# Expert stage: four expert outputs added onto x in one chain on VectorE instead of two accumulators and a join, with the routing set between the links

## What is computed

```python
def _L0_ffn_ref(x, router_w, router_b, expert_w, expert_b):
    router_probs = jax.nn.softmax(x @ router_w + router_b, axis=-1)
    top_p, top_i = jax.lax.top_k(router_probs, K)          # K = 2 of E = 8 experts
    top_p = top_p / jnp.sum(top_p, axis=-1, keepdims=True)
    expert_out = jnp.einsum('bnd,edc->bnec', x, expert_w) + expert_b
    gathered = jnp.take_along_axis(expert_out, top_i[..., None], axis=2)
    return jnp.einsum('bnk,bnkc->bnc', top_p, gathered)
...
t = t + _L0_ffn_ref(_ln_t(t), L0_ffn_router_w, L0_ffn_router_b, L0_ffn_expert_w, L0_ffn_expert_b)
```

## Time and profile before

| | before |
|---|---|
| median of 3 runs | 10527.13 us (10521.58 to 10538.14) |
| the profiled execution's own time | 10524.25 us |
| its span, first to last instruction | 10522.5 us |
| busy in the span: PE, DVE, ACT, POOL | 82%, 65%, 50%, 56% |
| the expert stage in it | about 2191 to 4327 us |
| busy in that stretch: PE, DVE, ACT, POOL | 1761, 1857, 1095, 1572 of 2136 us |

### The profile page before, as it was taken

The page is one execution under the profiler, slowest core; times in us unless marked ns, Lnnn a source line. Parts: engine busy times, 40 slices in busy tenths (PEclk is TensorE's granted clock), DMA queues, the critical chain, the costliest instruction groups (busy, mean ns, idle before and its releaser), DMA issues. The chain is left out here.

```text
span 10522.5 us, 333676 instructions
## 1 busy us (share of the span) xinstructions
PE 8609.7 (82%) x109757; PEld 5525.2 (53%) x109757; DVE 6874.4 (65%) x22569; ACT 5282.8 (50%) x14181; POOL 5917.0 (56%) x7369
## 2 busy tenths in 40 slices
PE   7888888878888888677759999995666668888888
PEld 5666666633333333355535555555666655555554
DVE  7888888878888888777725555556778772222222
ACT  4555555545555555566634444444666653333333
POOL 7777777767777777666612222224555554444444
PEclk9999999989999999888879999997888889999999
DMA  1111111111111111498943444437888862222222
GB/s 48 49 49 49 49 49 50 50 48 50 50 48 47 50 50 46 93 178 177 177 135 156 161 158 158 158 129 127 145 142 144 137 110 54 56 56 56 56 56 54
DMA packets 1199080, 961.46 MB, mean 91 GB/s; under 512 B 338169, under 2 KB 1078457, under 8 KB 1190202
## 3 DMA queue, kind: packets, MB, share of 16 engines
q1 hardware_dynamic: 1198522, 956.38, 36.8%
HBM read 576.97 MB, written 455.45 MB: 98 GB/s over the span
## 5 line engine op out<-in xcount | busy, mean ns | idle before, releaser
L943 PE MATMUL moe_pe_out<-moe_we,moe_xnT 128*128 128x512 f32 x3136 | 1531.6, 623 | 373.0 <-DVE moe_odd L836 197.2
L1533 PE MATMUL conv_pc<-conv_c,conv_toep 128*128 128x432 f32 (+1 forms) x3584 | 1370.5, 535 | 0.0
L740 ACT ACTIVATE moe_scaled<-moe_pe_out,moe_gate 128x128 f32<-128x128 f32 x3136 | 891.9, 367 | 867.6 <-PE moe_pe_out L943 865.8
L2092 ACT ACTIVATE rec_yT<-rec_ph 128x32 f32<-128x32 f32 x3136 | 618.5, 197 | 1241.7 <-PE rec_ph L2213 1241.7
L1384 POOL TENSOR_TENSOR conv_g<-conv_c,conv_gate 128x896 f32<-128x896 f32 x128 | 365.1, 2852 | 1462.9 <-DVE conv_out L1496 1362.8
L943 PEld LDWEIGHTS moe_pe_out<-moe_we,moe_xnT 128*128 128x128 f32 x3136 | 557.3, 195 | 1188.3 <-issue 1187.2
L2213 PE MATMUL rec_ph<-rec_yT,rec_vt 128*32 128x32 f32 x25080 | 843.1, 207 | 196.5 <-ACT rec_yT L2092 121.7
L1533 PEld LDWEIGHTS conv_pc<-conv_c,conv_toep 128*128 128x128 f32 x3584 | 672.1, 190 | 599.1 <-issue 599.1
L2139 DVE COPY rec_xT<-rec_pin 128x512 f32<-128x512 f32 x196 | 135.6, 692 | 1240.9 <-PE rec_pin L2185 1240.9
L281 POOL TENSOR_SCALAR att_xn<-att_xin,att_mv,att_rstd 128x128 f32<-128x128 f32 x1024 | 868.2, 857 | 54.1 <-POOL att_rstd L277 54.1
L678 POOL TENSOR_TENSOR moe_paired<-moe_scaled 128x256 f32<-128x256 f32 x784 | 569.3, 726 | 537.2 <-ACT moe_scaled L740 521.5
(11 more groups left out here) (194 smaller groups left out, 21904.3 us busy)
## 6 DMA issues: line engine op xcount, KB each, us to landing
conv_toep<-rows_dram SPq DMA_DIRECT2D x32, 2304.0 KB, 12.6
c<-foc_cs SPq DMA_DIRECT2D x32, 1856.0 KB, 12.0
conv_cin<-c SPq DMA_DIRECT2D x32, 1856.0 KB, 7.5
x<-att_x1s SPq DMA_DIRECT2D x3584, 14.0 KB
ctx_all<-conv_out SPq DMA_DIRECT2D x32, 1792.0 KB, 5.7
att_xin<-x_windows SPq DMA_DIRECT2D x512, 98.0 KB
moe_xin<-x SPq DMA_DIRECT2D x112, 448.0 KB, 3.5
x<-moe_acc SPq DMA_DIRECT2D x112, 448.0 KB, 2.7
```

What stands on the lines that cost most here:

```text
L740: ins = act.activation(scaled[:, b, e, :], pe_out[:, b, 1, e * C:(e + 1) * C], ACT.Identity, scale=g)
L943: ins = pe.matmul(pe_out[:, b, half, :], xnT[:, n.slot(2), t, :], we[:, half * 4:half * 4 + 4, :].rearrange("d e c -> d (e c)"), start=Tru ...
L1533: ins = pe.matmul(pc[k][:, half, 0:HALF * wide].rearrange("p (b i) -> p b i", i=wide)[:, :, i0:i1], w, tile[:, n.slot(slots), b, i0 + away ...
L2092: act.activation(yT[:, a, cs], ph[:, a, cs], ACT.Sigmoid).then_inc(moved, 1)
```

## The change

It takes away the accumulator `odd` and its join: experts 0, 1, 2, 3 are added onto x in `acc` one after another, each waiting for the one before with a `hold` on `mixing`. `add_others` of the tile before moves up, directly behind the first of the four. The 15 routing steps go one behind each of the four, from tile 2, place 0, on (k = 4(t-2)+place), and end in tile 5. ACT's `shares` moves from behind tile 2 to behind tile 3. The statistics of group n+3 are spread over the places of tile 6, and the rest of them follows it.

```diff
--- before.py
+++ after.py
@@ -588,7 +588,6 @@
         part = S.sb("part", [P, 2, T, E])
         gate = S.sb("gate", [P, 2, T, E])
         acc = S.sb("acc", [P, 4, T, C])
-        odd = S.sb("odd", [P, 2, C])
         scaled = S.sb("scaled", [P, 2, 4, C])
         paired = S.sb("paired", [P, 2, 2, C])
         others = S.sb("others", [P, 2, C])
@@ -610,7 +609,7 @@
         routing = S.sem("routing")
         shares_ready = S.sem("shares_ready")
         expert_done = S.sem("expert_done")
-        mixing, joined, mixed = S.sem("mixing"), S.sem("joined"), S.sem("mixed")
+        mixing, mixed = S.sem("mixing"), S.sem("mixed")
         scaled_ready, paired_ready, others_ready = S.sem("scaled_ready"), S.sem("paired_ready"), S.sem("others_ready")
         x2_out = S.sems("x2_out", 4)
         block = S.block()
@@ -752,7 +751,7 @@
                     if last < -1:
                         if t == 0:
                             front(n + 1, first)
-                        if t == 2:
+                        if t == 3:
                             shares(n + 1)
                     if t == 4 and last < -2:
                         norm(n + 2)
@@ -823,64 +822,45 @@
                     ins = dve.tensor_tensor(gate[:, n.slot(2), :, :], part[:, 0, :, :], part[:, 1, :, :], ALU.add)
                 ins.then_inc(routing, 1)
 
-            def route_between(n, t, place, more):
-
-                k = 6 * (t - 1) + place - 4
-                if more and 0 <= k < ROUTE_OPS:
+            def between(n, t, place, last):
+
+                k = 4 * (t - 2) + place
+                if last < -1 and 0 <= k < ROUTE_OPS:
                     route(n + 1, k)
-
-            def gated(n, t, e, into, start=False, onto=None):
-                g = gate[:, n.slot(2), t, e:e + 1]
-                src = pe_out[:, (n.off * T + t) % 2, 0, e * C:(e + 1) * C]
-                if start:
-                    dve.tensor_scalar(into, src, g, None, ALU.mult).then_inc(mixing, 1)
-                else:
-                    dve.scalar_tensor_tensor(out=into, in0=src, scalar=g, in1=into if onto is None else onto, op0=ALU.mult, op1=ALU.add)\
-                       .then_inc(mixing, 1)
-
-            def mix(n, t, first, more):
-
-
-                b = (n.off * T + t) % 2
-                if first >= 1 or t >= 2:
-                    hold(dve, joined, n.val(T, t - 1), ticks)
+                if last < -3 and t == T - 1:
+                    if place == 0:
+                        layer_stats(n + 3, 0, 1)
+                    layer_stats(n + 3, place + 1, place + 2)
+
+            def gated(n, t, e):
+                a = acc[:, n.slot(4), t, :]
+                dve.scalar_tensor_tensor(out=a, in0=pe_out[:, (n.off * T + t) % 2, 0, e * C:(e + 1) * C],
+                                         scalar=gate[:, n.slot(2), t, e:e + 1], in1=a if e else xin[:, n.slot(4), t, :],
+                                         op0=ALU.mult, op1=ALU.add).then_inc(mixing, 1)
+
+            def mix(n, t, first, last):
+
+
                 if t == 0:
                     hold(dve, routing, n.val(ROUTE_OPS, ROUTE_OPS), ticks)
+                    if first >= 4:
+                        hold(dve, x2_out[n.slot(4)], n.turn(4, 16), ticks)
                 dve.wait_ge(expert_done, n.val(T, t + 1))
-                gated(n, t, 1, odd[:, b, :], start=True)
-                route_between(n, t, 0, more)
-                if t == 0 and first >= 4:
-                    hold(dve, x2_out[n.slot(4)], n.turn(4, 16), ticks)
-                gated(n, t, 0, acc[:, n.slot(4), t, :], onto=xin[:, n.slot(4), t, :])
-                route_between(n, t, 1, more)
-                if first >= 1 or t >= 1:
-                    add_odd(n, t - 1)
-                route_between(n, t, 2, more)
-                hold(dve, mixing, n.val(T * MIX, MIX * t + 1), ticks)
-                gated(n, t, 3, odd[:, b, :])
-                route_between(n, t, 3, more)
-                if first >= 1 or t >= 1:
-                    add_others(n, t - 1)
-                route_between(n, t, 4, more)
-                hold(dve, mixing, n.val(T * MIX, MIX * t + 2), ticks)
-                gated(n, t, 2, acc[:, n.slot(4), t, :])
-                route_between(n, t, 5, more)
-
-            def tile_of(n, t):
+                for e in range(MIX):
+                    if e:
+                        hold(dve, mixing, n.val(T * MIX, MIX * t + e), ticks)
+                    gated(n, t, e)
+                    if e == 0 and (first >= 1 or t >= 1):
+                        add_others(n, t - 1)
+                    between(n, t, e, last)
+
+            def add_others(n, t):
 
                 m, u = (n, t) if t >= 0 else (n - 1, T - 1)
-                return acc[:, m.slot(4), u, :], (n.off * T + t) % 2
-
-            def add_odd(n, t):
-                a, b = tile_of(n, t)
+                a = acc[:, m.slot(4), u, :]
                 hold(dve, mixing, n.val(T * MIX, MIX * (t + 1)), ticks)
-                dve.tensor_tensor(a, a, odd[:, b, :], ALU.add).then_inc(joined, 1)
-
-            def add_others(n, t):
-                a, b = tile_of(n, t)
-                hold(dve, joined, n.val(T, t + 1), ticks)
                 dve.wait_ge(others_ready, n.val(T, t + 1))
-                dve.tensor_tensor(a, a, others[:, b, :], ALU.add).then_inc(mixed, 1)
+                dve.tensor_tensor(a, a, others[:, (n.off * T + t) % 2, :], ALU.add).then_inc(mixed, 1)
 
             def step(n, first, last):
                 if first == 0:
@@ -893,20 +873,15 @@
                         layer_stats_end(n + k)
                     for k in range(ROUTE_OPS):
                         route(n, k)
-                more = last < -1
                 for t in range(T):
-                    mix(n, t, first, more)
+                    mix(n, t, first, last)
                     if last < -2 and t == 2:
                         negate(n + 2)
-                    if last < -3 and t == 5:
-                        hold(dve, normed, n.val(TP, 2 * TP), ticks)
-                        layer_stats(n + 3, 0, 4)
-                    if last < -3 and t == 6:
-                        layer_stats(n + 3, 4, T)
-                if not more:
-                    add_odd(n, T - 1)
+                if last == -1:
                     add_others(n, T - 1)
                 if last < -3:
+                    layer_stats(n + 3, MIX + 1, T)
+                    hold(dve, normed, n.val(TP, 2 * TP), ticks)
                     layer_stats_end(n + 3)
 
             run_steps(dve, N, U, step, 4)
```

## The result

| | before | after |
|---|---|---|
| median | 10530.71 us (4 runs, 10521.58 to 10538.14) | 10756.29 us (4 runs, 10745.58 to 10759.79) |
| ratio, 95% interval | | 1.0213 [1.0195, 1.0231] |
| span of the profiled execution | 10522.5 us | 10752.9 us |
| expert stage, first expert matmul to last operation | 2137 us | 2360 us |
| the other five stages together, PE's first to last in each | 8123 us | 8134 us |

The kernel became 226 us slower, where 104 us were forecast. The sign and the first cause were right; the size was not, and 10756 us lies outside the range of 10504 to 10700. Nearly all of it is in the stage that was changed: of the 230 us between the two profiled executions 222 are there, and the other five stages grew by 11 together.

A forecast was written before the change was run, and what follows sets the result against it. A ring of PE, DVE's work and PE two tiles on bounds the expert stage. Groups of 19.05 against 18.18 us cost 97 us over 112, back edges 7; 104 on 10524 gives 10628 us, range 10504 to 10700.

The forecast's parts named there:

- the first cause: Expert stage, tiles 3 and 5: `add_others`, moved to second place, makes DVE wait for POOL's half, ready 3.30 us after ACT began.
- if L863 finds POOL's half ready in most tiles: Sign in the profile after that would prove the forecast wrong: `add_others` (L863) not waiting for POOL in most tiles.
- the pair that was named against rival B: Expert stage: DVE's busy time down by 220 us or more while the stage gets longer.
- rival B: DVE's load counts, so fewer operations make the kernel faster: group 16.25 us, 10308 us; chance 0.18 with partial forms.
- Links: DVE's chain of gated operations: each waits for the one before, 0.49 us start to start, bounds 0.37 and 0.49.
- rival A: Chained links cost only 0.26 us each, so the stage stays as long as now, 10518 to 10525 us; chance 0.12.
- The sum: One group from tile 2's matmuls: PE restarts at 13.52, plus 5.75 makes 19.27 us with both collisions; 19.05 taken against 18.18.
- I take the mean of the two ends of the second: Tile 5: step 12's collision with POOL's next addition, called close, counted at half, 19.27 less 0.22 us.
- The base: Group length before the change that the sum is compared with: 18.18 us, mean of three groups away from the back edge.
- At the 25 back edges DVE is late and its tile 0 is on the path: Loop's back edge: the chain needs 1.81 us where the alternation needed 1.52; 0.29 times 25, 7 us.
- Rival C: Worse than the sum: tile 6 holds PE up at the next group's tile 1, 10675 us and up; chance 0.12.
- The statistics and the moved sigmoids: Statistics only shift within and behind tile 6, thinly covered; sigmoids come one tile later, ACT's tile 4 0.22 us after they begin.

The follow-up runs named there:

- experiment 1: Kernel after with `add_others` moved from behind the first to behind the third of the four links: 10540.9 us, ratio 1.0017 to the kernel before.
- experiment 6: Kernel after with `add_others` behind the third link and the chain's waits bare instead of `hold`: 10439.4 us, ratio 0.9913 to the kernel before.
- experiment 7: Kernel after with four unused matmuls of 128 columns added on PE behind tiles 2 to 6: 10671.5 us, ratio 1.0135 to the kernel before.
- experiment 4: Kernel after with 40 increments of an unused counter ahead of DVE's loop, moving its code: 10724.9 us, ratio 1.0192 to the kernel before.
- experiment 2: Kernel after with the routing step put ahead of `add_others` instead of behind it: 10657.8 us, ratio 1.0128 to the kernel before.
- experiment 5: Kernel after with `add_others` behind the third link and 40 increments ahead of DVE's loop: 10632.0 us, ratio 1.0097 to the kernel before.

## Why the prediction was wrong in size

**The mechanism: right.** DVE waits for POOL's half in the tiles where that was forecast: 1.40 us a group, of which 0.85 in tile 5 and 0.35 in tile 3. It had not before, and moving `add_others` back takes nearly the whole loss away (experiment 1). One sign was badly put: "if L863 finds POOL's half ready in most tiles" would have made the forecast wrong, and it does find it ready in 503 of 784, but the forecast itself named two tiles of seven. DVE's busy time fell while the stage grew, the pair that was named against rival B; only the fall is 41 us and not 220, because an operation in a chain counts its whole length and because those that meet POOL's take up to 0.8 us. The forecast of that number had left both out. Experiments 1 and 6 show that rival B was no mere slip: with the late place the chain with fewer operations is indeed worth something, 38 us away from the edge and 91 in all with bare waits on top, but not 216, and not in the order that this change has.

**Links.** Taken at 0.49, measured at 0.50 with `hold` and 0.38 with the bare wait, which was the bound taken from below (0.37). So rival A, with links of 0.26, fell. The Trainium skill, VectorE: DVE Perf Modes, section on the drain that can't be avoided, has it that a semaphore after each operation costs nothing extra. The trace agrees for raising one: every gated operation here raises `mixing`, and an independent one still follows after 0.27 us (3014.92 to 3015.19 in the kernel after). The prediction took it for waits as well, and there the trace does not agree: even the bare wait for the operation before costs 0.12 us more than 0.26.

**The group: right in kind, too small.** The sum had 13.52 + 5.75, less 0.22 for half a collision, 19.05. The rows gave 13.69 + 5.87, so 19.56, and the collision of step 12 is there in full. The most frequent length over the stage is 19.53. That is 1.22 us above the 18.31 of before, times 87, 106 us, where the forecast had 0.87 x 87 = 76. Of the 0.51 us between 19.05 and 19.56 the step "I take the mean of the two ends of the second" is 0.22: in the rows above the end of POOL's half starts both engines' next additions within 0.1 us of each other, so that they meet is the rule here (107 of 112). The other 0.29 are 0.17 from tile 2 to PE's restart and 0.12 in tiles 0 and 1, which no step of the sum explains. The base was off too: the three groups of the earlier trace rows gave 18.18, the stage 18.31, which takes 0.13 back.

**The clock: not in the sum.** The mean of the 87 groups is not 19.53 but 19.97, since about a quarter of them last 21.13 like the one above. 0.44 x 87 is 38 us. Waits of PE for DVE, which the forecast itself lengthened, precede the 1.2 GHz stretches. The sum priced PE as if it ran at 2.4 GHz throughout, as the earlier trace rows had it with 0.98. Experiment 7 removes those stretches away from the edge (2 us are left of 83) together with most of PE's waits for DVE (112.5 us between 2250 and 4250, of 443.0) and is faster, which fits but does not measure it alone.

**The back edge: the step that failed.** The sentence was "At the 25 back edges DVE is late and its tile 0 is on the path", with 0.29 each, 7 us; besides, those groups got the 0.87 of every group. So 1.16 x 24 = 28 us were forecast (24 edges, not 25) and 3.20 x 24 = 77 came. 2.01 of the 3.20 are the idle time that grew from 3.02 to 5.03 us; the other 1.19 are what was forecast. Experiment 4 shows that the edit itself does not need it: with 40 idle instructions ahead it is gone. The row of the edge showed a stop of 3.18 us, and the prediction treated it as a constant of the loop, though the change rewrites the code whose fetching it is. In all thirteen kernels the stop goes with the fetches: 3.0 to 3.1 us where one piece has landed before DVE starts again, 5.0 to 5.1 where two have.

Put together: 49 us at the edges, 38 us by the clock and 30 us in the chain are the 117 us between 104 and 221. No single one would have taken the result out of the range; with the group's own error alone it would have come near 10660.

**Rival C** (tile 6 holds the next group's tile 1) does not show: PE's row at 3018.22 for that tile has no wait. **The statistics and the moved sigmoids** were costed at nothing and in the sum respectively; ACT's tile 4 follows the sigmoids at 3029.34, 0.22 us after they began, as forecast.

## What to carry to other kernels

Put a wait for another engine's late result where the fewest of your own operations queue behind it, not where the data flow lists it; here the position of one 0.2 us addition was worth more than all the operations saved. When DVE waits for POOL, put no operation with two large operands in SBUF next if POOL's next addition is ready, since it starts within 0.1 us of the same event (experiment 2). And when the code of a hardware loop changes its length, look at the idle time of its back edge before believing any difference of a few us a pass, in later stages too; a few idle instructions ahead tell it apart from real work.

## What was not expected of the hardware

- The idle time of an engine at a hardware loop's edge depends on where the code lies: 3.02 us before, 5.03 after, 3.05 with the same body moved by 40 instructions. It goes with the number of 8 KB fetches that land before the restart (one or two, 2.4 us apart). In a stage with DMA at 0.78, stops of 11.2 us on average were seen instead, in a loop that fetched no code again in any other run.
- An increment of a semaphore behind a wait costs 0.12 us of queue time in a dependent chain (0.50 against 0.38 from start to start). The increment that an operation makes at its own end costs nothing that shows (0.27 to the next independent one).
- A DVE addition of 128x128 with two operands in SBUF lasts 0.28 us alone and 0.80 to 0.84 when POOL's addition began 0.04 to 0.07 us ahead. When DVE is first it keeps its 0.29, and POOL's goes from 0.73 to 0.77.
- More work on PE made the kernel faster (experiment 7): it filled waits, and away from the edge the granted clock stayed at 1.00, which is 38 us of the 85.

What stays open: why the code's move in experiment 5 hits the later stage and the same move in experiment 4 does not (the two programs differ by one instruction of DVE a pass besides the place of `add_others`), what makes the other 48 us of experiment 7, why a slow stretch of PE follows some waits and not others, and the 0.29 us of the group that the sum does not explain.
